# A block of zeros ahead of each landed chunk: a TensorE filler in the last message pass of a fused graph network

## The chip, the cores and the metric

The kernel runs on one core of one Trainium2 chip. The metric is the device time of one execution in microseconds (us), lower is better. The kernel before takes 6255.49 us (median of 3 runs, 6251.28 to 6260.96).

Five engines work side by side, each on its own instruction stream, and meet at semaphores: TensorE (matmuls, PE in the profile, its weight loads PEld), VectorE (DVE), ScalarE (ACT), GpSimd (POOL) and SyncE (SP), which here only issues transfers.

## The reference

Four graph layers over the same 3125 nodes of 128 features and 100000 edges, the edges sorted by destination, each followed by a residual and a layer norm:

```
x = layernorm(x + relu(three R-GCN convolutions(concat(x, type_embedding))))
x = layernorm(x + elu(layernorm(attention sums(x)) * w + b))
x = layernorm(x + (segment_sum(edge_weight * x[src], dst) @ W.T + b))            # L2
x = layernorm(x + mlp(concat(x, segment_sum(edge_attr, dst) / max(count, 1))))   # L3
```

The change touches the code that does the sums of L2 and L3, which the kernel makes in one pass over the edges.

## The kernel before, in words

Nodes are padded to 25 tiles of 128. The edges lie in chunks of 128 along the sorted destinations, and U = 6 chunks make a group. A tile of destinations is the work of several groups. A sum over the edges of a tile is a row of matmuls that accumulate in a PSUM bank: one operand is a one-hot matrix (edge by destination in the tile, times a weight), the other the 128 gathered message rows of the chunk.

There are four such message passes, numbered k = 0 to 3: one for each R-GCN convolution (k = 0, 1, 2), and the last (k = 3), which has 147 groups, 882 chunks. Passes 1 and 2 count edges between nodes as well, with four bf16 matmuls of 400 columns for each chunk (`count_sources`, L1440). Between pass 2 and pass 3 stand the attention layer and two dense stages; behind pass 3 the dense stages of the MLP.

For one group p of pass 3 the engines do this:

- GpSimd (`gather`, L493) starts one indirect DMA for each of the 6 chunks. It fetches 128 rows of `z_tab` into slot q of `msg_r`, by the row numbers in `idx_r[:, q]`. Ahead of slots 0 and 3 it waits until that half of the slots has been freed by TensorE (`s_free`) and has new row numbers (`s_idx`). There is one buffer for each slot.
- ScalarE (`rows_to_gather`, L578) waits until slot q has landed and then copies the row numbers of the next group to `idx_r[:, q]`. At a tile's end it also takes the tile's two sums out of PSUM (L686, L687).
- SyncE (L431) loads the edge attributes of the chunk into the other half of the slot once TensorE has freed it; `s_attr` tells that they landed.
- VectorE makes the group's columns (L876, L882) and then, for each half of three slots, the one-hots (`one_r`, a view of `shot_r`, L893) and the weighted one-hots (`hot_r`, L897), once the half is free.
- TensorE (`group_sums` with `chunk3`) waits at slots 0 and 3 for the one-hots (`s_hot`), at every slot for the gathered rows (`s_msg`) and the attributes (`s_attr`), and then does two fp32 matmuls: attributes by one-hots (L1580) and messages by weighted one-hots (L1581, which frees the slot). The trace lists each fp32 matmul as two matmuls with two weight loads. A tile begins with `start3` (L1575, L1576 and a clearing matmul of zeros, L1203) and ends with closing matmuls of zeros (L1207).

The accumulators of pass 3 are banks 0 to 3, two for each of two tiles in turn. `zeros_b` is a bf16 block of zeros, [128, 512], filled once at the start. Bank 5 isn't used in pass 3.

Of the kernel before, what the change touches and what calls it, by code (L numbers as in the profile page):

```python
# [18 lines left out]
P = 128  # L19
# [32 lines left out]
def build(nc, x_nodes, x_t, src_c, dst_c, typ_c, wgt_c, dst_rows, attr, node_type, emb, w1, root1, w2, root2,  # L52
          w3, b1r, b2r, emb_parts, gat_w, l2_w, m_w1, m_w2, rows, out):
    ctx = ExitStack()
    with ctx:
        def sb(name, shape, dt=F32):
            return ctx.enter_context(nc.sbuf_tensor(name, shape, dt))
# [23 lines left out]
        zeros_b = sb("zeros_b", [P, 512], BF16)  # L81
# [56 lines left out]
        psum = ctx.enter_context(nc.psum_tensor("psum", [P, 8, 512], F32))  # L138
# [1061 lines left out]
        def _(pe):  # L1200
            T = nc.tensor
# [25 lines left out]
            for n, (of, by) in enumerate(((0, ident), (1, ident), (1, before))):  # L1227
                T.matmul(psum[0:1, 6, 32 * n:32 * n + 32], rng_col[:, of:of + 1], by[0:TILES, 0:32], start=True, stop=True)
                last = T.matmul(psum[0:1, 6, 32 * n + 96:32 * n + 128], rng_wcol[:, of:of + 1], by[0:WN, 0:WN],
                                start=True, stop=True)  # L1230
# [73 lines left out]
            def transpose_relations(p):  # L1304
                pe.wait_ge(s_cols[0], p)
                T.matmul(psum[0:SPLIT * SPLIT_AT, 2, 0:P], rel_g[:, :, :].rearrange("p i n -> p (i n)"), ident_b[:, :], start=True, stop=True).then_inc(s_rel_ps, 1)

            def inverse_counts(p, slot):

                alone(pe)  # L1310
                pe.wait_ge(s_rel_t, p)
                for h in range(2):
                    T.matmul(psum[:, 6 + h, 0:UH * P], rel_t[:, :],
                             inv_b[:, bass.ds(slot, 1), h * UH * P:(h + 1) * UH * P].rearrange("p o n -> p (o n)"),
                             start=True, stop=True).then_inc(s_inv_e[h], 1)

            def group_sums(k, p, slot, chunk_sums, first=False, last=False):
                after, landed = pe.snap(p + 1), pe.snap(p * 16)
                if k == 0:
                    inverse_counts(p, slot)  # L1320
                for q in range(U):
                    if q % UH == 0:
                        pe.wait_ge(s_hot[k][q // UH], after)
                    pe.wait_ge(s_msg[k][q], landed)
                    if k == 3:
                        pe.wait_ge(s_attr[q], landed)
                    chunk_sums(q, slot, first and q == 0, last and q == U - 1).then_inc(s_free[k], 1)
                    if k == 0 and q == UH:
                        transpose_relations(after)
# [4 lines left out]
            def gathering(k, start, chunk_sums, stop, between=None, after=None, begin=1, tab=rest):  # L1334


                def tile(D, slot):
                    first, last = pe.snap(tile_range(pe, P0, D, tab)), pe.snap(tile_range(pe, LAST, D, tab))
                    start(D, slot)
                    group_sums(k, first, slot, chunk_sums, first=True)  # L1340
                    if between is not None:
                        between(D)
                    with pe.Fori(first + 1, last) as p:
                        group_sums(k, p, slot, chunk_sums)
                    group_sums(k, last, slot, chunk_sums, last=True)
                    if after is not None:
                        after(D)
                    stop(slot)

                tile(begin, begin % 2)  # L1350
                with pe.Fori(begin + 1, TILES) as D:
                    tile(D, pe.snap(D % 2))
# [292 lines left out]
```

## Time and profile before

| | |
|---|---|
| median of 3 runs | 6255.49 us (6251.28 to 6260.96) |
| the profiled execution | 6247.44 us, span of its instructions 6245.6 us |
| mean granted TensorE clock | 0.756 |
| busy share of the span | TensorE 71%, GpSimd 52%, VectorE 48%, ScalarE 17% |
| pass 0, about 730 to 2000 us | clock 0.72 |
| pass 1, about 2030 to 3140 us | clock 0.94 |
| pass 2, about 3190 to 4290 us | clock 0.95 |
| pass 3, about 4720 to 6060 us | clock 0.52 |

The span runs from the first to the last instruction. The granted clock is the share of TensorE's full rate (2.4 GHz) that it was given, and it has two levels, 0.5 and 1.0; a value between them is a mean over a stretch. Busy time is the time in which an engine had an instruction in work. Matmuls are pipelined, and the end of one is modelled, so the start of the next is the safer reading. A row of waits says for what an engine stood idle and how often. The prediction counts the passes from one: k = 1 and 2 are the second and third pass, k = 3 is the last.

### The profile page before, as it was taken

The page shows a single profiled execution, that of the slowest core. Times are in us where ns is not written, and L with a number is a line of the kernel's source. Part 1 is how long each engine was busy: PE and PEld are TensorE (multiplying, and loading weights), DVE is VectorE, ACT ScalarE, POOL GpSimd, SP SyncE. Part 2 cuts the span into 40 slices and gives each one's busy share as a digit, 9 for nine tenths or more (in the row PEclk, how much of TensorE's full clock was granted, in tenths as well). Part 3 has the DMA queues.
Part 4 walks back from the last instruction along what each step waited for, and adds up shares of the span by engine and source line. Part 5 has one row for each costly group of instructions (what it writes and reads, how often), then busy time and mean ns, then how long its engine had stood idle before and what let it go on. Part 6 is the DMA issues. An engine that isn't in the chain of part 4 may idle for free.

```text
span 6245.6 us, 98864 instructions
## 1 busy us (share of the span) xinstructions
PE 4417.3 (71%) x20570; PEld 3106.2 (50%) x20573; DVE 2981.6 (48%) x6741; ACT 1057.7 (17%) x3779; POOL 3267.3 (52%) x3114
## 2 busy tenths in 40 slices
PE   4677676767677777777767777775647777877773
PEld 1223455555565445454544444444645665666652
DVE  5443222222222666667666666666882222222235
ACT  0111111111111111111111111111751111111112
POOL 0000355555554666666666666663325666666650
PEclk7566667777777999999999999997985555555556
DMA  1011223333333122222222222222423333333320
GB/s 67 23 53 53 79 85 93 102 92 102 95 104 106 53 61 72 71 81 81 90 74 61 65 71 77 82 79 74 147 94 85 85 85 85 84 84 85 84 73 11
DMA packets 318265, 492.02 MB, mean 79 GB/s; under 512 B 98090, under 2 KB 221228, under 8 KB 314556
## 3 DMA queue, kind: packets, MB, share of 16 engines
q0 software_dynamic: 108864, 246.74, 14.6%
q1 hardware_dynamic: 209372, 244.94, 11.8%
q8 instruction: 12, 0.20, 0.0%
q14 instruction: 17, 0.14, 0.0%
HBM read 406.11 MB, written 85.29 MB: 79 GB/s over the span
## 4 chain that ended last, share of the span: by engine, by line
issue 24%; POOL 22%; PE 19%; DMA 12%; DVE 9%; another core or an unknown queue 6%; DVEq 3%; ACTq 2%; ACT 2%; POOLq 1%; SPq 0%
POOL msg_r L493 22%; DMA msg_r<-y_tab,idx_r 8%; PE psum L1375 4%; DMA msg_r<-z_tab,idx_r 3%; PE psum L1440 3%; DVE h_t L1132 2%; PE psum L1255 1%; PE psum L1580 1%; DVE hot_r L990 1%; PE psum L1287 1%; PE psum L1267 1%; PE psum L1537 1%; ACT idx_r L578 1%; PE psum L1581 1%
## 5 line engine op out<-in xcount | busy, mean ns | idle before, releaser
L493 POOL DMA_INDIRECT msg_r<-y_tab,idx_r x2160 | 2234.6, 1035 | 2053.2 <-issue 1291.3
L1440 PE MATMUL psum<-shot_r,hotb_r 128*128 128x400 bf16 x5760 | 1313.6, 353 | 573.3 <-DMA msg_r<-y_tab,idx_r 454.8
L493 POOL DMA_INDIRECT msg_r<-z_tab,idx_r x882 | 933.6, 1058 | 511.5 <-issue 323.1
L1440 PEld LDWEIGHTS psum<-shot_r,hotb_r 128*128 128x128 bf16 x5760 | 503.4, 102 | 1009.4 <-DMA msg_r<-y_tab,idx_r 489.2
L1014 DVE TENSOR_SCALAR shot_r<-iota_h,edge_g 128x1600 bf16<-128x1600 f16 x1440 | 906.1, 684 | 0.0
L578 ACT COPY idx_r<-row_i 128x1 int32 x2142 | 409.9, 191 | 2898.6 <-DMA msg_r<-y_tab,idx_r 2643.2
L1580 PE MATMUL psum<-msg_r,shot_r 128*128 128x128 f32 x1764 | 680.2, 488 | 294.3 <-DMA msg_r<-z_tab,idx_r 152.1
L1375 PE MATMUL psum<-hot_r,msg_r 128*128 128x128 f32 x2880 | 634.5, 385 | 319.8 <-DVE hot_r L990 193.9
L1375 PEld LDWEIGHTS psum<-hot_r,msg_r 128*128 128x128 f32 x2880 | 540.9, 277 | 434.3 <-issue 260.9
L1580 PEld LDWEIGHTS psum<-msg_r,shot_r 128*128 128x128 f32 x1764 | 437.2, 308 | 522.8 <-DMA msg_r<-z_tab,idx_r 351.0
L893 DVE TENSOR_TENSOR shot_r<-iota_h,dst_g 128x384 f32<-128x384 f16 x294 | 166.1, 565 | 862.7 <-PE psum L1581 436.7
L1581 PE MATMUL psum<-msg_r,hot_r 128*128 128x128 f32 x1764 | 551.3, 416 | 0.0
L893 DVE TENSOR_TENSOR hotb_r<-iota_h,dst_g 128x384 bf16<-128x384 f16 x480 | 266.5, 555 | 551.1 <-PE psum L1462 226.6
L1581 PEld LDWEIGHTS psum<-msg_r,hot_r 128*128 128x128 f32 x1764 | 474.2, 328 | 0.0
L990 DVE SCALAR_TENSOR_TENSOR hot_r<-iota,edge_g,psum 128x128 f32<-128x128 f32 x720 | 202.9, 344 | 487.0 <-remote 271.6
L578 ACT COPY idx_r<-src_i 128x1 int32 x876 | 167.6, 191 | 1145.9 <-DMA msg_r<-z_tab,idx_r 967.4
L1462 PEld LDWEIGHTS psum<-hot_r,msg_r 128*128 128x128 f32 x1440 | 278.6, 203 | 60.0 <-issue 13.6
L1495 PEld LDWEIGHTS psum<-msg_r,hot_r 128*128 128x128 f32 x1440 | 277.5, 202 | 59.0 <-issue 12.3
L1462 PE MATMUL psum<-hot_r,msg_r 128*128 128x128 f32 x1440 | 291.3, 286 | 0.0
L1495 PE MATMUL psum<-msg_r,hot_r 128*128 128x128 f32 x1440 | 290.4, 285 | 0.0
L897 DVE TENSOR_TENSOR hot_r<-hotb_r,edge_g 128x384 f32<-128x384 bf16 x480 | 283.0, 590 | 0.0
L1564 PE MATMUL psum<-side,h_t 128*128 x1250 | 170.6, 295 | 77.1 <-POOL h_t L513 52.8
(273 smaller groups left out, 3905.3 us busy)
## 6 DMA issues: line engine op xcount, KB each, us to landing
msg_r<-in_attr SPq DMA_DIRECT2D x882, 64.0 KB
h_t<-count_tab SPq DMA_DIRECT2D x25, 1600.0 KB, 6.6
count_tab<-w_s SPq DMA_DIRECT2D x48, 800.0 KB
msg_r<-y_tab,idx_r POOLq DMA_INDIRECT x2160
xn<-heavy_tab SPq DMA_DIRECT2D x76, 320.0 KB
y_tab<-y_s SPq DMA_DIRECT2D x25, 640.0 KB, 2.9
xn<-y_tab SPq DMA_DIRECT2D x25, 640.0 KB
y_tab<-y_s SPq DMA_DIRECT2D x50, 320.0 KB
```

The lines of the kernel that those rows point to most:

```text
L493: pool.indirect_dma_start(out=msg_r[:, q, 0:width], out_offset=None, in_=table, in_offset=bass.IndirectOffsetOnAxis(ap=idx_r[:, q:q + 1], ...
L578: nc.scalar.copy(idx_r[:, q:q + 1], of[:, q:q + COLS - U + 1][:, bass.ds(c0, 1)]).then_inc(s_idx[k], 1)
L893: return V.tensor_tensor(out=to, in0=iota_h[:, None, 0:P].broadcast_to(shape), in1=dst_g[:, part, None].broadcast_to(shape), op=ALU.is_equal)
L897: return V.tensor_tensor(out=to[:, half, :], in0=ones_in[:, half, :], in1=edge_g[:, plane, half, None].broadcast_to([P, UH, P]), op=ALU.mult)
L990: last = V.scalar_tensor_tensor(out=hot_r[:, q, :], in0=iota[:, 0:P], scalar=edge_g[:, DST, q:q + 1], in1=psum[:, 6 + h, (q - half.start) ...
L1014: V.tensor_scalar(out=shot_r[:, q, :], in0=iota_h[:, :], scalar1=edge_g[:, SRC, q:q + 1], scalar2=None, op0=ALU.is_equal)
L1375: last = T.matmul(acc0(slot, m), msg_r[:, q, m * P:(m + 1) * P], hot_r[:, q, :], start=False, stop=False)
L1440: ins = T.matmul(psum[:, 4 + b, 0:CB], hotb_r[:, q, :], shot_r[:, q, b * CB:(b + 1) * CB], start=first, stop=last)
L1462: return T.matmul(acc(slot), msg_r[:, q, 0:P], hot_r[:, q, :], start=False, stop=False)
L1495: return T.matmul(acc(slot), hot_r[:, q, :], msg_r[:, q, 0:P], start=False, stop=False)
L1580: T.matmul(acc(slot * 2 + 1), one_r[:, q, :], msg_r[:, q, P:2 * P], start=False, stop=False)
L1581: return T.matmul(acc(slot * 2), hot_r[:, q, :], msg_r[:, q, 0:P], start=False, stop=False)
```

## The change

In the last pass alone (k = 3), TensorE multiplies the block of zeros by itself, 128x128 weights and 512 moving columns in bf16, into bank 5, once for each slot. The matmul stands behind the wait for the one-hots and ahead of the wait for the gathered rows. It increments no semaphore, and nothing reads its result.

```diff
@@ -1321,6 +1321,8 @@
                 for q in range(U):
                     if q % UH == 0:
                         pe.wait_ge(s_hot[k][q // UH], after)
+                    if k == 3:
+                        T.matmul(psum[:, 5, :], zeros_b[:, 0:P], zeros_b[:, :], start=True, stop=True)
                     pe.wait_ge(s_msg[k][q], landed)
                     if k == 3:
                         pe.wait_ge(s_attr[q], landed)
```

## Rows read from the trace of the kernel before

**Rows 1.** The page: busy time of each engine, and the clock in 40 slices (tenths).
```profile
PE 4417.3 (71%) x20570; PEld 3106.2 (50%) x20573; DVE 2981.6 (48%) x6741; ACT 1057.7 (17%) x3779; POOL 3267.3 (52%) x3114
...
PEclk7566667777777999999999999997985555555556
```

**Rows 2.** Sums by pass: length, PE, PEld, DVE, ACT, POOL busy, clock, DMA, GB/s.
```profile
730.00:2000.00 1270.00, 902.87 (x4387) 731.76 (x4388) 316.80 (x1886) 164.86 (x767) 703.65 (x700) 0.72 0.32 97
2030.00:3140.00 1110.00, 840.22 (x4539) 545.86 (x4538) 762.19 (x1459) 181.28 (x820) 739.52 (x707) 0.94 0.25 74
3190.00:4290.00 1100.00, 809.75 (x4550) 536.24 (x4549) 751.25 (x1449) 157.47 (x746) 735.34 (x701) 0.95 0.25 72
4720.00:6060.00 1340.00, 1056.42 (x3627) 814.49 (x3626) 384.57 (x864) 175.68 (x912) 915.24 (x865) 0.52 0.31 85
```

**Rows 3.** Line 493, last pass: duration of a gather in ns, minimum/median/maximum.
```profile
L493 POOL DMA_INDIRECT msg_r<-z_tab,idx_r x865: 994/1000/1387, 4719.2 to 6059.0; - x173
```

**Rows 4.** Timeline, last pass: start and length in us, engine, line, [idle before, releaser].
```profile
5508.49 0.79 PE L1580 MATMUL psum<-msg_r,shot_r 128*128 128x128 f32 x2
...
5509.08 0.64 PE L1581 MATMUL psum<-msg_r,hot_r 128*128 128x128 f32 x2
5509.77 1.00 POOL L493 DMA_INDIRECT msg_r<-z_tab,idx_r  x1 [0.30 <-issue]
...
5511.07 1.00 POOL L493 DMA_INDIRECT msg_r<-z_tab,idx_r  x1 [0.30 <-issue]
...
5512.32 0.79 PE L1580 MATMUL psum<-msg_r,shot_r 128*128 128x128 f32 x2
...
5512.91 0.63 PE L1581 MATMUL psum<-msg_r,hot_r 128*128 128x128 f32 x2
5513.69 1.00 POOL L493 DMA_INDIRECT msg_r<-z_tab,idx_r  x1 [0.30 <-issue]
...
5516.18 0.56 DVE L893 TENSOR_TENSOR shot_r<-iota_h,dst_g 128x384 f32<-128x384 f16 x1 [5.22 <-PE psum L1581]
...
5516.95 1.25 POOL L493 DMA_INDIRECT msg_r<-z_tab,idx_r  x1 [2.27 <-ACT idx_r L578]
```

**Rows 5.** GpSimd's waits, last pass, 4720 to 6060: us in total, times, longest.
```profile
POOL msg_r L493 <- ACT idx_r L578: 127.3, 60, 2.6
POOL msg_r L493 <- PE psum L1581: 55.2, 33, 2.8
```

**Rows 6.** The same for the second pass, 2030 to 3140.
```profile
POOL msg_r L493 <- ACT idx_r L578: 107.1, 51, 3.2
POOL msg_r L493 <- PE psum L1462: 54.6, 29, 4.2
```

**Rows 7.** Timeline of TensorE in the second pass, at the full clock.
```profile
3001.20 0.85 PE L1440 MATMUL psum<-shot_r,hotb_r 128*128 128x400 bf16 x4 [0.37 <-DMA msg_r<-y_tab,idx_r]
3001.88 0.38 PE L1462 MATMUL psum<-hot_r,msg_r 128*128 128x128 f32 x2
```

**Rows 8.** Line 1203, matmuls of zeros ahead of the attention sums, ns.
```profile
L1203 PE MATMUL psum<-zeros_b x3: 314/634/634, 4379.7 to 4380.6; 128*128 128x512 bf16 x2, 128*128 128x128 bf16 x1
```

**Rows 9.** Timeline of TensorE behind a tile boundary of the last pass.
```profile
5500.37 0.63 PE L1580 MATMUL psum<-msg_r,shot_r 128*128 128x128 f32 x2
...
5501.22 0.63 PE L1580 MATMUL psum<-msg_r,shot_r 128*128 128x128 f32 x2
...
5502.33 0.49 PE L1580 MATMUL psum<-msg_r,shot_r 128*128 128x128 f32 x2 [0.19 <-DMA msg_r<-z_tab,idx_r]
5502.65 0.39 PE L1581 MATMUL psum<-msg_r,hot_r 128*128 128x128 f32 x2
```

**Rows 10.** Sums of the stretches around it (columns as in rows 2).
```profile
5497.50:5501.80 4.30, 4.30 (x21) 4.18 (x21) 0.59 (x2) 0.38 (x2) 2.62 (x3) 0.50 0.23 61
5501.90:5505.20 3.30, 0.95 (x6) 0.57 (x5) 2.39 (x6) 0.77 (x4) 1.77 (x2) 1.00 0.28 75
```

**Rows 11.** The chain of waits from 4716 to 6070, shares by line.
```profile
by line: POOL msg_r L493 34.7%; issue 31.3%; DMA msg_r<-z_tab,idx_r 15.8%; PE psum L1580 6.7%; PE psum L1581 3.8%; ACTq L578 1.9%; ACT idx_r L578 1.8%; POOLq L486 0.7%; ACTq L245 0.7%; another core or an unknown queue 0.6%; ACTq L577 0.6%; 
```

## The prediction

> **What bounds the kernel now.** I read the page first, then sums by pass, then the last pass alone. The page [rows 1] shows TensorE busy most of the time and, in the last quarter, a granted clock of only 5 tenths (1.2 GHz) where the passes before had 9. The sums by pass [rows 2] show the puzzle of this case: in the last message pass TensorE is busy 1056 of 1340 us (79%) at clock 0.52, in the second and third pass it is busy 74 to 76% at 0.94 and 0.95, and still all three take the same time for a gather: 1340/865 = 1.549 us, 1110/707 = 1.570 us, 1100/701 = 1.569 us. Nearly twice the clock bought nothing there per gathered chunk.
>
> The reason is GpSimd. One gather of the last pass takes 1.00 us [rows 3], and the next starts 0.30 us later (5509.77, 5511.07 [rows 4]), so 1.30 us is the floor: 882 x 1.30 = 1147 us of the pass. What lies above the floor are waits [rows 5]: 60 on ScalarE's index copy (127.3 us) and 33 on L1581 (55.2 us), together 93 waits and 182.5 us, 2 us each. The second pass has the same kind at the same price: 51 + 29 waits, 161.7 us [rows 6]; per gather that is 0.229 us there and 0.211 us here.
>
> What ends such a wait? In rows 4, slot 2 of a group is multiplied at 5508.49 to 5509.72. GpSimd needs that slot's release only for the gather begun at 5511.07, and is busy with the one before until 5510.77: about 1.0 us of slack. The next half group is the one that stalls, 2.27 us, until 5516.95. The chunk whose slot it needs (slot 5 of the same group) started at 5512.32 and its last matmul ended at 5512.91 + 0.63 = 5513.54, before GpSimd had even issued the gather before (5513.69 to 5514.69). So the multiply was not late; the release reached GpSimd, ScalarE and VectorE (VectorE started L893 at 5516.18) some 2.6 us after its matmul. The profile puts the wait down to ScalarE's index copy, which follows the landing of the gather begun at 5513.69: the stall ended when the last gather under way had landed. A faster matmul moves none of this. I read most of the 93 waits so.
>
> **The change, part by part.** Nothing is removed or moved. Six matmuls of 128x512 bf16 zeros with their weight loads are added to each of the 147 groups, 882 in all, into bank 5, which nothing in this pass reads (it accumulates in banks 0 to 3).
>
> Size of one: at the full clock four matmuls of 400 columns step at (3001.88 - 3001.20)/4 = 0.17 us [rows 7], so 512 columns take 0.22 us, and at half the clock 0.43 us; the row with the same form lists 0.63 us for one alone [rows 8], drain included. Added work: 882 x 0.43 = 379 us cold, 882 x 0.22 = 194 us warm, more than the pass's 284 us of idle TensorE only if everything stayed cold.
>
> What hides it: supply is one chunk in 1.30 us. Back to back a cold chunk takes 0.85 us (L1580 at 5500.37, again at 5501.22 [rows 9]), so 0.45 us are free and 0.43 us go in. Alone, from its landing, a cold chunk takes 5508.49 to 5509.72 = 1.23 us, of which the first part is the weight load, which can run under the zeros.
>
> What it does to the clock: behind a tile boundary, from 5497.5 to 5501.8, TensorE ran back to back at 0.50, and right behind it, at 5501.9, the clock was 1.00 [rows 9, 10]. With the zeros in, a cold pass is always back to back (0.85 + 0.43 = 1.28 of 1.30 us). That zeros count as work I take from the second and third pass: there most columns are one-hots against one-hots, nearly all zeros, and the clock is 0.94. I expect 0.8 to 0.95 in the last pass. A warm chunk takes 5502.33 to 5503.04 = 0.71 us [rows 9] where a cold one takes 1.23 us, so each release comes 0.52 us earlier.
>
> What that is worth:
> - The 60 ACT waits and the steady state: nothing, by the paragraph above. If the cover were gone (gathers faster than 1.28 us), each chunk would cost up to 0.43 us.
> - The 33 waits on L1581: bounds 0 and 33 x 0.52 = 17 us. A few of them look like matmuls in a row with GpSimd behind them, others like the stall above; I take half, -8 us.
> - More instructions on a warm TensorE: the second and third pass have 4539/707 = 6.4 matmuls a gather, this one 4.2, and cost 0.020 us more a gather, 18 us over 882. One more matmul of those 2.2 would be 8 us; VectorE's extra work there may be all of it, so the bounds are 0 and 18 us and I take +4 us.
> - The tail: the last chunk ends 0.5 us earlier, and a tile's close too: -1 us.
> Sum -5 us. The profiled execution took 6247.4 us around its span of 6245.6, 8 us (0.13%) under the median of 6255.5; -5 us on it is 6242, and on the median, by which I forecast, 6250 us.
>
> The Trainium skill, "Trace Analysis", section "Matmul Optimizations", says that TensorE's power follows its utilization, so that matmuls should run back to back. The rise behind the tile boundary [rows 10] agrees; that zeros do it no run here shows yet. Taken as a recipe for time, with every matmul of the last pass at twice the rate and the gain all on the path, it would give the first rival's 6184 us; the sum does not use it.
>
> **Rivals.**
> *A, the clock reaches the path (faster).* The chain of waits gives L1580 and L1581 6.7% + 3.8% of the last pass's stretch of 1354 us [rows 11], 142 us. If these are true steps, halving the matmuls takes 71 us: 6184 us. If only the stalls on L1581 vanish, 55 us: 6200 us. For it: the chain and 55.2 us of waits. Against: the second and third pass have the warm clock and as many waits.
> *B, zeros do not raise the clock and are in the way (slower).* At 0.50 the chunk plus zeros needs 1.28 of 1.30 us, so the backlog that a tile boundary leaves no longer drains. The boundary's own two fp32 matmuls are worth a chunk, 0.85 us, and its three small zero matmuls some 0.35 us (an estimate from the 0.43 us of one with 512 columns): 1.2 us behind, against 1.0 us of slack. 25 tiles x (0.2 + 0.43) = 16 us; if each of the 93 waits is lengthened by 0.43 too, 40 us more. Between 16 and 56 us I take the middle, +35 us: 6290 us. It decides from the point where the clock stays below about 0.6. Against: the zeros-heavy columns of the second and third pass.
> *C, warm, but the waits become those of the second and third pass (slower).* There a gather costs 0.020 us more than here, and in the second pass 0.018 us more of it is waiting. With TensorE as warm and fuller, the term of +4 us becomes its upper bound of 18 us and the -8 us nothing: 18 - 1 = +17 us, 6272 us. It decides if the stall comes from TensorE's instruction rate. Against: with 4.2 matmuls a gather instead of 6.4 the difference is that small, and VectorE alone can be its cause.
> *D, the clock does not rise, and all is hidden.* Then nothing changes: 6255 us. It falls within my forecast's own range.
>
> **How the numbers follow.** A measurement of this kernel (6251 to 6261) can tell about 0.2% (12.5 us) from no change. Forecast with D 0.53, own range 6240 to 6267; A 0.25; B 0.11; C 0.11. Faster 0.25, same 0.53, slower 0.22. For 8 in 10, I go down to A's smaller price, 6200 (about 0.1 is left below), and up to 6285 (C's price with 13 us over it, and B's lower end of 6271; about 0.08 is left above). 6250 is that of the likeliest case.
>
> **What the profile after should show.** The last pass's clock at 0.8 or more; 882 more TensorE matmuls; L1581's and L1580's spacing halved in most groups; GpSimd's gathers still 1.30 us apart with stalls of about 2 us every 9 to 12 gathers, on ScalarE's copy more than on L1581; the pass within 10 us of its length. The forecast is wrong if the number of stalls changes clearly: fewer would mean that TensorE's releases, held back as they look, depend on how busy or fast it is (A), more that added instructions feed the stall (C). A clock near 0.5 with longer waits on L1581 would be B.

## The result, and the profile after

The changed kernel takes 6270.28 us (median of 17 runs, 6255.65 to 6278.24), the kernel before 6255.49 us beside it. The ratio is 1.0021, with a 95% interval of 1.0013 to 1.0028: slower by 14.8 us in the median (8 to 18 us by the interval), where 6250 was forecast. The profiled execution took 6275.3 us around a span of 6273.5.

The page after (lines as in [rows 1]):

```profile
PE 4325.8 (69%) x21402; PEld 2935.0 (47%) x21455; DVE 2979.0 (47%) x6741; ACT 1057.5 (17%) x3779; POOL 3255.8 (52%) x3114
...
PEclk7566666777778999999999999997988888888876
```

The sums by pass (columns as in [rows 2]; the third pass left out):

```profile
730.00:2000.00 1270.00, 898.11 (x4342) 726.88 (x4342) 315.12 (x1879) 163.84 (x763) 701.80 (x699) 0.73 0.32 96
2030.00:3140.00 1110.00, 837.86 (x4527) 544.16 (x4526) 760.86 (x1459) 180.61 (x817) 736.75 (x704) 0.94 0.25 73
...
4720.00:6060.00 1340.00, 946.56 (x4394) 632.56 (x4442) 382.11 (x854) 173.78 (x903) 894.08 (x858) 0.83 0.31 84
```

The page shows 882 more weight loads (21455 for 20573). In the last row of the sums the granted clock went from 0.52 to 0.83, and TensorE is busy for 947 us instead of 1056, with the zeros in. The other passes are as they were in clock and busy time. So the clock did what was forecast. But in the same 1340 us GpSimd began 858 gathers instead of 865.

One gather costs what it did, and the zeros are listed at 0.38 us. Line 493 in the last pass (as in [rows 3]):

```profile
L493 POOL DMA_INDIRECT msg_r<-z_tab,idx_r x858: 992/997/1382, 4719.6 to 6059.8; - x172
```

The line of the zeros:

```profile
L1325 PE MATMUL psum<-zeros_b x809: 379/379/634, 4721.9 to 6059.6; 128*128 128x512 bf16 x162
```

The time is in GpSimd's waits. Its waits in the last pass, which answer to [rows 5] (L1583 is the old L1581):

```profile
POOL msg_r L493 <- ACT idx_r L578: 113.0, 54, 2.6
POOL msg_r L493 <- PE psum L1583: 101.2, 49, 2.4
```

Those of the second pass, which answer to [rows 6]:

```profile
POOL msg_r L493 <- ACT idx_r L578: 120.2, 59, 3.2
POOL msg_r L493 <- PE psum L1464: 45.6, 28, 4.7
```

In the last pass there were 93 waits of 182.5 us; there are 103 of 214.2 us, still some 2 us each. Those put down to ScalarE fell from 60 to 54, and those put down to TensorE's last matmul rose from 33 to 49, although that matmul now comes earlier.

The whole pass, counted from its 882 gathers (from the start of the first to the end of the last; "idle" is what the gaps between gathers have beyond the usual 0.304 us; a stall is a gap over 0.9 us):

```
          pass us   gathers busy    idle   stalls
before    1365.5       933.6       164.0      93
after     1379.7       920.2       191.5     103
```

The last pass is 1379.7 - 1365.5 = 14.2 us longer in these two profiles. The idle time grew by 27.5 us, and the gathers became 13.4 us shorter in all; the last section comes back to that.

One profile is too little to take this for the 14.8 us of the result. The two profiled executions differ by 27.9 us, and the other half of that lies in passes whose code did not change. Over six profiles beside a kernel before of about 6256 us (before, the change, and the four runs of the first set below) the unchanged first pass takes 1312 to 1327 us and has 97 to 106 such stalls. So the loss is shown by the medians of many executions, and a step from 93 to 103 stalls is hardly more than what single profiles scatter by.

The chain of waits over the last pass (as in [rows 11]):

```profile
by line: POOL msg_r L493 37.3%; issue 28.7%; DMA msg_r<-z_tab,idx_r 19.1%; PE psum L1582 3.9%; PE psum L1583 2.7%; PE psum L1325 1.3%; ACT idx_r L578 1.3%; ACTq L578 1.2%; another core or an unknown queue 0.8%; POOLq L486 0.8%; ACTq L245 0.
```

The timeline of one stall (as in [rows 4]):

```profile
5501.82 0.49 PE L1582 MATMUL psum<-msg_r,shot_r 128*128 128x128 f32 x2 [0.88 <-DMA msg_r<-z_tab,idx_r]
...
5502.14 0.39 PE L1583 MATMUL psum<-msg_r,hot_r 128*128 128x128 f32 x2
...
5502.49 1.00 POOL L493 DMA_INDIRECT msg_r<-z_tab,idx_r  x1 [0.30 <-issue]
...
5504.59 0.56 DVE L893 TENSOR_TENSOR shot_r<-iota_h,dst_g 128x384 f32<-128x384 f16 x1 [4.43 <-PE psum L1583]
...
5505.10 0.49 PE L1582 MATMUL psum<-msg_r,shot_r 128*128 128x128 f32 x2 [0.32 <-DMA msg_r<-z_tab,idx_r]
...
5505.37 1.24 POOL L493 DMA_INDIRECT msg_r<-z_tab,idx_r  x1 [1.88 <-PE psum L1583]
```

A chunk now takes 0.71 us (5501.82 to 5502.53), as forecast for a warm TensorE. Its shares of the chain fell from 6.7% + 3.8% to 3.9% + 2.7%, those of the gather and its transfer rose, and the pass did not become shorter. The stall is the one of [rows 4]. VectorE and GpSimd both need the slots freed by 5502.53. VectorE starts 2.06 us later, and GpSimd 2.84 us later. A release that is due is held back.

The trace's records of semaphore updates show this directly. In the stall of [rows 4] the matmuls that release slots ended at 5512.27, 5513.54, 5514.91 and 5516.26, and the updates of `s_free` stand at 5516.08, 5516.15, 5516.21 and 5516.28, in a burst. GpSimd started 0.80 us behind the second, which is the one that it needed. In the stall above they ended at 5502.53, 5503.35 and 5504.57, the updates stand at 5504.56, 5504.63 and 5504.70, and GpSimd started 0.81 us behind the first. In the traces of after_3 and narrow1_3, from chips without these stalls (below), each of the 882 updates stands 0.014 us behind the end of its matmul, and a GpSimd that waits for one starts 0.82 us after that end.

So it goes for nearly all stalls of the pass. GpSimd waits at slots 0 and 3, where 92 of the 93 stalls before and 102 of the 103 after lie. In all of them the matmul that it needed had ended at least 1.2 us before the restart, and 87 of the 92 and 95 of the 102 restarts come 0.79 to 0.83 us behind a recorded update of `s_free` (of the other gathers at these slots 11 of 200 and 4 of 190 do). The same test with ScalarE's `s_idx` gives 2 and 0. The stalls end with TensorE's release, whichever engine the profile names, and not with a gather's landing, as the prediction read one of them. From the end of the needed matmul to the restart the median is 3.17 us before and 3.72 us after: the matmul is some 0.5 us earlier, and the release is held that much longer.

### The profile page after: what moved, and what is told of

Read it like the earlier page. It is cut to its first block, busy times and chain, and to the rows that moved or that the text cites. A ratio compares the mean times of both kernels' runs of the same rounds, so it can differ in the third digit from the quotient of the medians.

```text
span 6273.5 us, 100578 instructions
## 1 busy us (share of the span) xinstructions
PE 4325.8 (69%) x21402; PEld 2935.0 (47%) x21455; DVE 2979.0 (47%) x6741; ACT 1057.5 (17%) x3779; POOL 3255.8 (52%) x3114
## 4 chain that ended last, share of the span: by engine, by line
issue 23%; POOL 23%; PE 20%; DMA 14%; DVE 8%; another core or an unknown queue 6%; DVEq 3%; ACT 1%; ACTq 1%; POOLq 1%; SPq 0%
POOL msg_r L493 23%; DMA msg_r<-y_tab,idx_r 9%; PE psum L1377 4%; DMA msg_r<-z_tab,idx_r 4%; PE psum L1442 4%; DVE h_t L1132 2%; PE psum L1255 1%; PE psum L1287 1%; DVE hot_r L990 1%; PE psum L1267 1%; PE psum L1539 1%; PE psum L1582 1%; PE psum L1497 1%; DVE h_t L1136 1%
## 5 line engine op out<-in xcount | busy, mean ns | idle before, releaser
L493 POOL DMA_INDIRECT msg_r<-z_tab,idx_r x882 | 920.2, 1043 | 539.0 <-issue 318.1
L1582 PE MATMUL psum<-msg_r,shot_r 128*128 128x128 f32 x1764 | 494.1, 370 | 376.8 <-DMA msg_r<-z_tab,idx_r 308.4
L1582 PEld LDWEIGHTS psum<-msg_r,shot_r 128*128 128x128 f32 x1764 | 344.4, 234 | 670.5 <-DMA msg_r<-z_tab,idx_r 573.7
L1583 PE MATMUL psum<-msg_r,hot_r 128*128 128x128 f32 x1764 | 412.4, 323 | 0.0
L1325 PE MATMUL psum<-zeros_b 128*128 128x512 bf16 x832 | 381.2, 458 | 24.0 <-DVE hot_r L897 19.1
L1583 PEld LDWEIGHTS psum<-msg_r,hot_r 128*128 128x128 f32 x1764 | 341.6, 241 | 0.0
L1497 PEld LDWEIGHTS psum<-msg_r,hot_r 128*128 128x128 f32 x1440 | 280.5, 204 | 59.5 <-issue 13.0
L1497 PE MATMUL psum<-msg_r,hot_r 128*128 128x128 f32 x1440 | 292.8, 287 | 0.0
L897 DVE TENSOR_TENSOR hot_r<-hotb_r,edge_g 128x384 f32<-128x384 bf16 x480 | 281.5, 587 | 0.0
```

What stands on the lines that cost most here:

```text
L493: pool.indirect_dma_start(out=msg_r[:, q, 0:width], out_offset=None, in_=table, in_offset=bass.IndirectOffsetOnAxis(ap=idx_r[:, q:q + 1], ...
L897: return V.tensor_tensor(out=to[:, half, :], in0=ones_in[:, half, :], in1=edge_g[:, plane, half, None].broadcast_to([P, UH, P]), op=ALU.mult)
L1325: T.matmul(psum[:, 5, :], zeros_b[:, 0:P], zeros_b[:, :], start=True, stop=True)
L1497: return T.matmul(acc(slot), hot_r[:, q, :], msg_r[:, q, 0:P], start=False, stop=False)
L1582: T.matmul(acc(slot * 2 + 1), one_r[:, q, :], msg_r[:, q, P:2 * P], start=False, stop=False)
L1583: return T.matmul(acc(slot * 2), hot_r[:, q, :], msg_r[:, q, 0:P], start=False, stop=False)
```

## The experiments

Each kernel is compared with the kernel before beside it on its own chip, and times are not compared across chips. This matters, since the chips differ more than the kernels. One chip has the 2 us stalls (kernel before: 6255.98 us in one session, 6171.06 in a second). Three others have nearly none in the last pass (5609.22, 5611.27 and 5627.04 us, 10% less). For the first comparison, of the result above, the chip is not on record; its times and stalls are those of the chip with stalls.

The questions: does the clock buy anything, does added work cost by its time or by its number of instructions, and must they be TensorE's?

### First set, on the chip with the stalls

**narrow1**: the same instructions as in the change, with 8 columns instead of 512.

```diff
+                    if k == 3:
+                        T.matmul(psum[:, 5, 0:8], zeros_b[:, 0:P], zeros_b[:, 0:8], start=True, stop=True)
```

> The zeros matmul of each slot is kept but has 8 columns instead of 512: the same 882 extra instructions pairs, almost no work. Count theory (GpSimd's stall of 2 us comes more often with every instruction on TensorE's stream): clock stays at 0.52 in the last pass, stalls over 0.9 us there rise from 93 to about 103, time +13 us, 6268 us. Clock theory (the higher clock makes the stalls more frequent): 93 stalls, 6255 us. Queue theory (512 columns of zeros stand ahead of landed chunks): 93 stalls, 6255 us.

**narrow3**: three of them for each slot.

```diff
+                    if k == 3:
+                        T.matmul(psum[:, 5, 0:8], zeros_b[:, 0:P], zeros_b[:, 0:8], start=True, stop=True)
+                        T.matmul(psum[:, 5, 0:8], zeros_b[:, 0:P], zeros_b[:, 0:8], start=True, stop=True)
+                        T.matmul(psum[:, 5, 0:8], zeros_b[:, 0:P], zeros_b[:, 0:8], start=True, stop=True)
```

> Three zeros matmuls of 8 columns in each slot, 2646 extra ones with little work. Count theory: stalls in the last pass rise by about three times as many as with one, to 115 to 125, time +30 to +40 us. Clock and queue theory: little change, under +8 us.

**vector12**: nothing on TensorE; behind the one-hots of each half VectorE increments a semaphore six times, 12 in a group. It does no work.

```diff
+                        for _ in range(UH * 2):
+                            dve.sem_inc(s_go, 1)
```

> Nothing on TensorE; instead 12 increments of a semaphore nobody waits for in each group on VectorE's stream in the last pass, behind its one-hots, as many added instructions as the weight loads and matmuls of the change. If the count theory holds for any engine's instructions (a path that all share): stalls 93 to about 103, +13 us. If it holds for TensorE alone, or the clock or queue theory holds: 93 stalls, 6255 us.

**wide_half**: the 512 columns of the change at slots 0 and 3 alone, a third of the instructions.

```diff
+                    if k == 3 and q % UH == 0:
+                        T.matmul(psum[:, 5, :], zeros_b[:, 0:P], zeros_b[:, :], start=True, stop=True)
```

> The 512-column zeros only at slots 0 and 3, 294 of them instead of 882. TensorE then has 0.85 + 0.14 us of cold work in 1.30 us, so the clock should be between, 0.6 to 0.75. Count theory: a third of the change's cost, +4 us, 96 stalls. Clock theory: in proportion to the clock, +5 to +9 us. Queue theory: +4 us.

Measured, with the gathers of the last pass counted as above in one profile each (the ratios are over 6 to 17 executions):

```
            added in the pass     clock  ratio (95%)               pass us  busy   idle  stalls
before      -                     0.52   1                          1365.5  933.6  164.0    93
wide_half   294 matmuls, wide     0.64   1.0001 (0.9992 to 1.0009)  1370.9  936.5  166.5    98
vector12    1764 increments       0.52   1.001  (1.0 to 1.002)      1375.7  930.6  177.2   103
narrow1     882 matmuls, narrow   0.52   1.0020 (1.0011 to 1.0028)  1376.8  941.9  166.9   101
after       882 matmuls, wide     0.83   1.0021 (1.0013 to 1.0028)  1379.7  920.2  191.5   103
narrow3     2646 matmuls, narrow  0.52   1.0044 (1.0032 to 1.0056)  1392.8  935.4  189.6   112
```

The sums of the last pass of narrow1:

```profile
4720.00:6060.00 1340.00, 1067.83 (x4454) 843.28 (x4453) 375.92 (x856) 174.12 (x904) 915.77 (x858) 0.52 0.30 84
```

Its waits of GpSimd:

```profile
POOL msg_r L493 <- ACT idx_r L578: 95.0, 47, 2.5
POOL msg_r L493 <- PE psum L1583: 92.8, 55, 2.4
```

GpSimd's waits in the last pass of vector12:

```profile
POOL msg_r L493 <- ACT idx_r L578: 147.8, 70, 2.8
POOL msg_r L493 <- PE psum L1583: 46.2, 36, 2.0
```

narrow1 settles the main question on this chip. It has the cold clock (0.52), adds hardly any columns, and costs what the change costs: 1.0020 against 1.0021. So clock and columns together are worth nothing that these runs can tell here (each interval is some 5 us to either side). What the columns cost and what the clock gives back are not told apart by it. In this pair of profiles the gathers of the change are 22 us shorter than those of narrow1, and its idle time is 25 us longer. Three times the instructions cost more than twice as much, with 112 stalls, and a third of them can't be told from none. Of the stall counts only the 112 stands clear of the 97 to 106 that the unchanged first pass has; narrow1's 101 does not, and its profile puts 8 us of its loss into longer gathers and 3 us into idle time. That narrow1's instructions cost time is shown; that they cost it through more stalls is not. vector12 has 103 stalls as well, with TensorE's code untouched, but at a ratio whose interval touches 1.0: it leans to "any engine's instructions" and doesn't settle it. For that a larger dose was needed.

### Second set, which fell on a chip without the stalls

**vector36**: as vector12, 36 increments in a group.

```diff
+                        for _ in range(UH * 6):
+                            dve.sem_inc(s_go, 1)
```

> 36 increments of an unread semaphore in each group on VectorE's stream in the last pass, three times the 12 of before; TensorE's stream is that of the kernel before. If instructions of any engine feed the stall: stalls in the last pass 110 or more, time +20 to +30 us. If TensorE's alone do and the +5 us of 12 increments was chance: 93 to 100 stalls, under +8 us. If VectorE is only late with its one-hots: longer waits on L897 by TensorE.

**attr_half**: fewer instructions. The attributes of three slots come in one transfer, and TensorE waits for them twice in a group instead of six times.

```diff
-                    for q in range(U):
-                        sp.wait_ge(s_free[3], p * U + (q + 1))
-                        sp.dma_start(msg_r[:, q, P:2 * P], attr[bass.ds((first_chunk(sp, p * U + chunk) + q) * P, P), :])\
-                          .then_inc(s_attr[q], 16)
+                    for q in range(0, U, UH):
+                        sp.wait_ge(s_free[3], p * U + (q + UH))
+                        sp.dma_start(msg_r[:, q:q + UH, P:2 * P],
+                                     attr[bass.ds((first_chunk(sp, p * U + chunk) + q) * P, UH * P), :]
+                                     .rearrange("(u n) f -> n u f", n=P)).then_inc(s_attr[q], 16)
...
-                    if k == 3:
+                    if k == 3 and q % UH == 0:
                         pe.wait_ge(s_attr[q], landed)
```

> The kernel before, but SyncE loads the attributes of three slots with one transfer (2 in a group instead of 6) and TensorE waits for them twice instead of six times: 4 DMA issues with their register work and 4 semaphore waits fewer in each group. Count theory for any engine: fewer stalls, 93 down to 80 to 88, time -10 to -25 us. Rival (the stall comes from TensorE's matmuls alone, or from the gathers): 93 stalls, 6255 us, or slower if the attributes now land too late.

**both_half**: that, and ScalarE copies the row numbers of three slots at once, in all four passes.

```diff
-                    for q in range(U):
...
-                        act.wait_ge(s_msg[k][q], before16)
-                        nc.scalar.copy(idx_r[:, q:q + 1], of[:, q:q + COLS - U + 1][:, bass.ds(c0, 1)]).then_inc(s_idx[k], 1)
+                    for q in range(0, U, UH):
...
+                        for j in range(UH):
+                            act.wait_ge(s_msg[k][q + j], before16)
+                        nc.scalar.copy(idx_r[:, q:q + UH], of[:, q:q + COLS - U + UH][:, bass.ds(c0, UH)]).then_inc(s_idx[k], 1)
```

> As attr_half, and ScalarE copies the row numbers of three slots at once (2 copies in a group instead of 6) in all four passes. Count theory for any engine: fewer stalls in every pass, 10 to 15% fewer each, time -60 to -100 us in all. Rival: the stalls stay as they are in the passes 0 to 2, time within 20 us of before; slower if the later row numbers bind GpSimd.

**no_attr**: the matmul of the attributes is left out, so the sums of L3 are missing from the output. It takes two of TensorE's four matmuls with their weight loads from each chunk.

```diff
-                T.matmul(acc(slot * 2 + 1), one_r[:, q, :], msg_r[:, q, P:2 * P], start=False, stop=False)
```

> The last pass leaves out the matmul of attributes by one-hots (L1580), so the attribute sums are missing from the output; the attributes are still loaded. TensorE loses 4 of its 8 matmul and weight load instructions a slot. Count theory: stalls in the last pass from 93 to 75 to 85, time -15 to -30 us. Rival (a stall has to do with gathers, not with how many instructions run beside them): 93 stalls, and only the tail's 1 us.

```
before 5609.22 us   ratio (95%)                pass us  busy   idle  stalls
vector36            1.0002 (0.999 to 1.0013)    1187.2  910.2   8.7     5
attr_half           1.0027 (1.0015 to 1.004)    1200.7  914.1  18.3    16
both_half           1.0014 (1.0004 to 1.0024)   1200.5  909.6  22.7    24
no_attr             0.994  (0.9922 to 0.9957)   1155.9  887.1   0.3     0
```

On this chip the pass takes some 1190 us instead of 1370, near the floor of 882 x 1.30 = 1147 us, nearly all stalls are gone (what is left has 0.7 us beyond the 0.30), and 5292 added increments (36 in each of 147 groups) cost nothing that can be measured. no_attr gains 34 us there, which says that TensorE's two matmuls per chunk do matter where no stall covers them. Grouping the transfers (attr_half) costs 15 us; that it lies in SyncE's wait for three freed slots and TensorE's for three attribute blocks is argued only. Both thinned kernels missed my expectation of a gain, and since neither ran on the chip with stalls, what they do there stays open.

### Third set: the same doses back on the chip with the stalls

> The changed kernel once more. If the kernel before takes about 6255 us beside it (stalls of 2 us in every pass, as in its profile): ratio 1.002 again, 103 stalls in the last pass. If it takes about 5609 us beside it (a chip without these stalls, as for the last four runs): the records theory (the stall comes of the recording of instructions, and the change costs only through it) expects no loss, and since GpSimd there waits 206 times, 64 us, for the last matmul of a slot, a gain of 10 to 50 us from the warm clock, 5560 to 5600 us. The count theory without records (each instruction costs by itself) expects +13 us there too, 5622 us.

> Three narrow zeros matmuls in each slot once more. On a chip with the stalls: 1.0044 again. On one without: the records theory expects 5609 us and up to +10 us where the narrow matmuls stand ahead of a slot that has landed, with the clock still near 0.55; the count theory +27 us.

> 36 unread increments on VectorE in each group once more. On a chip with the stalls: if instructions of any engine feed them, 110 or more stalls in the last pass, +15 to +30 us; if TensorE's alone, within 8 us. On one without: 5609 us again.

> The last pass without its matmul of the attributes (the attribute sums are missing from the output) once more. On a chip with the stalls: fewer instructions, 75 to 85 stalls in the last pass, -15 to -35 us. On one without: 0.994 again, -34 us, all of it from slots freed earlier.

```
before 6171.06 us   ratio (95%)                pass us  busy   idle  stalls
after_2             1.0021 (1.0011 to 1.0031)   1358.0  928.3  161.8    98
narrow3_2           1.0046 (1.003 to 1.0062)    1372.3  935.8  168.5   107
vector36_2          1.01   (1.0085 to 1.0115)   1402.1  922.6  211.7   133
no_attr_2           1.0062 (1.0046 to 1.0078)   1375.0  903.0  204.0    82
```

The sums of the last pass (4660 to 5900) of vector36_2:

```profile
4660.00:5900.00 1240.00, 798.57 (x3252) 664.14 (x3252) 341.28 (x777) 157.57 (x818) 815.02 (x780) 0.60 0.30 82
```

Its waits of GpSimd:

```profile
POOL msg_r L493 <- PE psum L1583: 88.3, 54, 3.7
POOL msg_r L493 <- ACT idx_r L578: 85.8, 48, 2.5
POOL msg_r L493 <- remote: 45.8, 25, 2.1
```

And what TensorE waited for by VectorE's weighted one-hots:

```profile
PE psum L1582 <- DVE hot_r L897: 130.3, 54, 5.8
```

The waits of GpSimd in no_attr_2, and one of TensorE's (L1580 is the old L1581):

```profile
POOL msg_r L493 <- ACT idx_r L578: 92.3, 35, 3.6
POOL msg_r L493 <- PE psum L1580: 91.0, 32, 6.1
PE psum L1580 <- DMA msg_r<-in_attr: 280.5, 154, 6.4
```

after_2 and narrow3_2 repeat their ratios. vector36_2 has the largest effect. Increments that wait for nothing and compute nothing, on an engine that is idle most of the pass, cost 57 us (1.0%) on this chip, where I had expected 15 to 30, with 133 stalls and 50 us more idle time than after_2. On the other chip they cost nothing (1.0002).

Its stalls are of two kinds, told apart by when the matmul that GpSimd needed ended (at slots 0 and 3; "us" is their time beyond 0.304 each):

```
             release held: matmul ended      matmul late: ended
             over 1.2 us before the restart  under 1.2 us before it
after_2      94, 154 us                      3, 5 us
narrow3_2    103, 163 us                     0
vector36_2   95, 148 us                      34, 55 us
no_attr_2    43, 90 us                       38, 110 us
```

VectorE's increments added no held releases (95 for 94). What they added is 34 stalls in which TensorE itself was late, in its wait for VectorE's one-hots (54 waits, 130.3 us, where after_2 has 19 waits of 5.4 us, at the zeros). VectorE was late by its increments: the 5255 of them that the trace lists took 348.5 us, 337 over 0.6 us each, where on the other chip 5256 took 110.4 us, 21 ns each and none longer. So on this chip another engine's instructions cost time as well, but in their own stream, and not by feeding the hold on TensorE's releases.

no_attr_2 is the miss of this set. With two matmuls and two weight loads fewer for each chunk the stalls did become fewer (82), but longer (2.45 us beyond the usual 0.30 on the mean, where the other three have 1.55 to 1.63), and the kernel is 38 us slower by its ratio. The table divides it. The held releases fell to less than half, 43 with 90 us, which is what a hold that comes with TensorE's instructions would give. In their place 38 stalls of 110 us came in which the matmul was late. There TensorE waited for the attributes, which this kernel still loads, 154 times and 280.5 us, a wait that after_2 doesn't have: SyncE began a chunk's load a median 5.5 us after the matmul that frees its slot, against 1.3 us in after_2 and 0.19 us in no_attr. Why SyncE fell so far behind here isn't shown.

### Fourth and fifth set: the clock, on chips without the stalls

> The changed kernel. Beside a kernel before of about 6170 or 6255 us (chip with stalls): 1.002 again. Beside one of about 5609 us (chip without): if the change costs only through the stalls, no loss and a gain of 10 to 50 us of GpSimd's 206 waits for TensorE; if an added instruction costs by itself, +13 us.

> One narrow zeros matmul in each slot, clock not raised. On a chip with stalls 1.002 again. On one without: 5609 us, within 8 us, so that a gain of the wide zeros there is the clock's.

> Attributes loaded and row numbers copied for three slots at once. On a chip with stalls, if instructions of any engine feed them: fewer stalls in all passes, -30 to -100 us; if only TensorE's and VectorE's do: within 15 us. On one without: 1.0014 again (later row numbers).

**both_half_zeros**: both_half, with the 512 columns of zeros for each slot as in the change.

> both_half with the change's zeros in it. On a chip with stalls: +10 to +15 us over both_half, as the change over before. On one without: 10 to 50 us below both_half by the warm clock.

> The 512-column zeros at slots 0 and 3 only. Beside a kernel before of about 5610 us (chip without stalls): the clock at 0.65 to 0.75 in the last pass and -10 to -20 us, about half of the change's gain. Beside one of about 6170 or 6255 us: 1.000 to 1.001, as the first time.

**mid128_4**: the change with 128 columns.

```diff
+                    if k == 3:
+                        T.matmul(psum[:, 5, 0:P], zeros_b[:, 0:P], zeros_b[:, 0:P], start=True, stop=True)
```

> A zeros matmul of 128 columns in each slot, a quarter of the change's columns with all of its instructions. Without stalls: the clock between 0.55 and 0.7, 0 to -10 us. With stalls: 1.002, as the change and its narrow form.

```
                  before us  clock  ratio (95%)                pass us  busy   idle  stalls
after_3            5611.27   0.99   0.9935 (0.9917 to 0.9953)   1153.9  882.4   3.2     4
narrow1_3          5611.27   0.54   1.0012 (1.0002 to 1.0022)   1201.1  911.1  21.8    16
both_half_3        5611.27   0.59   1.0009 (0.9998 to 1.0019)   1203.2  911.2  23.9    23
both_half_zeros    5611.27   0.98   0.9988 (0.9976 to 1.0)      1185.9  909.8   7.8     8
wide_half_4        5627.04   0.76   0.9946 (0.9926 to 0.9966)   1185.9  907.3  10.1     8
mid128_4           5627.04   0.69   0.9981 (0.9969 to 0.9993)   1200.3  920.4  11.6     7
```

The very same changed kernel is faster here, by 37 us. The sums of the last pass (4270 to 5390) of after_3:

```profile
4270.00:5390.00 1120.00, 797.46 (x4395) 493.15 (x4441) 373.60 (x856) 173.79 (x902) 856.08 (x857) 0.99 0.37 100
```

Its waits of GpSimd:

```profile
POOL msg_r L493 <- issue: 258.1, 847, 0.4
POOL msg_r L493 <- PE psum L1583: 5.3, 9, 1.0
POOL msg_r L493 <- ACT idx_r L578: 0.8, 1, 0.8
```

Then narrow1_3:

```profile
4270.00:5390.00 1120.00, 992.13 (x4266) 790.30 (x4267) 377.07 (x823) 167.03 (x867) 849.89 (x823) 0.54 0.35 96
```

Its waits of GpSimd:

```profile
POOL msg_r L493 <- issue: 185.7, 599, 1.0
POOL msg_r L493 <- PE psum L1583: 65.8, 203, 1.5
POOL msg_r L493 <- ACT idx_r L578: 19.0, 21, 1.3
```

Then wide_half_4:

```profile
4270.00:5390.00 1120.00, 834.96 (x3699) 630.24 (x3770) 370.58 (x832) 169.37 (x879) 856.91 (x834) 0.76 0.35 98
```

Its waits of GpSimd:

```profile
POOL msg_r L493 <- PE psum L1583: 29.3, 95, 0.6
POOL msg_r L493 <- ACT idx_r L578: 10.0, 13, 1.1
```

None of these waits is of the 2 us kind. And the 203 waits on L1583 in narrow1_3 are less than they look: 65.8 us is 0.32 us each, hardly more than the 0.30 us that GpSimd needs between two gathers anyway (the 847 of "issue" in after_3 take 0.30 us each). Beyond that a cold pass is idle for 21.8 us and a warm one for 3.2: 19 us, which I put down to TensorE's earlier releases. The larger part of the 47 us between these two passes is the gathers, 911.1 against 882.4, 29 us; the last section shows what makes them longer. The change's own instructions, narrow1_3, cost a few microseconds here (1.0012, 1 to 12 us by the interval), and its columns, through the clock, bring the rest. That interval overlaps with narrow1's on the chip with stalls (1.0011 to 1.0028), so up to all of narrow1's 12.5 us can be a cost that has nothing to do with the stalls.

Three fillers in the order of their clock, 0.69, 0.76 and 0.99, give 0.9981, 0.9946 and 0.9935 (the last on another chip). both_half_zeros brings both_half_3 down by 15 us only, although its clock is 0.98: its gathers stayed at 910 us.

The versions, on both kinds of chip:

```
             with stalls                       without
the change   1.0021, 1.0021                    0.9935
wide_half    1.0001 (0.9992 to 1.0009)         0.9946 (0.9926 to 0.9966)
narrow1      1.0020                            1.0012
```

wide_half_4 gained 30 us, more than the 10 to 20 that I had expected of it. wide_half is the version to keep. It is not measurably slower than the kernel before on the chip with the stalls, and takes most of the gain on the others (the two gains are from different chips, and their intervals overlap).

## Why the prediction was wrong

The range of 6200 to 6285 held the time, but not the sign. Point by point:

- **The clock** (0.8 to 0.95 forecast): 0.83. Right, and so was the step behind it, that zeros count as work: narrow1 with its 8 columns stayed at 0.52. The forecast that a warm chunk takes 0.71 us was right to the digit. Rivals B and D, which have the clock stay down, are out.
- **Zeros hidden in GpSimd's 1.30 us**: right as far as can be told. narrow1 and the change cost the same, so the 512 columns cost nothing that the clock did not give back.
- **The 60 waits on ScalarE's copy, worth nothing**: right in value (54 of them after), wrong in what ends them. The copy of [rows 4] was long done; the restart follows TensorE's held release (87 of 92 stalls).
- **The 33 waits on L1581, "I take half, -8 us"**: failed, measured nothing (1.0021 with the warm clock against 1.0020 without). They became 49. I had read the stall of [rows 4] as a release held back, and yet let half of these waits be matmuls that come late. The price of 2 us, the same as that of the other 60, was in [rows 5] and spoke for one kind. In none of the 92 stalls at slots 0 and 3 before, and in none of the 102 after, was the matmul late; when it ended 0.5 us earlier, its release was held 0.5 us longer.
- **"More instructions on a warm TensorE", +4 us with bounds 0 and 18**: mis-sized. narrow1 gives it alone, though at the cold clock: 1.0020 of 6256 is 12.5 us (7 to 18 us), and the whole change's +14.8 us lies within its interval. With +12.5 for +4 and 0 for -8 the sum of -5 becomes +11.5; either correction alone gives +3 to +3.5, within the noise, so it took both failures to get the sign and the size wrong. The upper bound of 18 us, from the second pass's extra matmuls, was the better value; I gave VectorE the benefit of the doubt, without a row that priced its part.
- **The tail, -1 us**: not resolved by any run. Instead of staying within 10 us of its length, the last pass grew by 14.2 us in the profile.
- **What would show it wrong**: "more that added instructions feed the stall (C)". The count came, 103 stalls for 93, but the unchanged first pass differs from one profile to another by nearly as much (97 to 106), so this sign could not have decided.

Rival C, given 0.11, forecast 6272 us, and 6270.28 was measured. That added TensorE instructions cost this much is shown (narrow1). Its condition, that the stall comes from TensorE's instruction rate, agrees with the large doses: 92 held releases before and 110 in narrow3 in the first session, 94 with the change and 43 with half of each chunk's matmuls left out in the second, though there late matmuls took the place of some. At the change's own dose it isn't told from the scatter, and narrow1_3 costs 1.0012 without any such stall. That C came within 2 us is luck. Its price had counted the waits of the second and third pass, not a measured dose. Against it I had put only that the passes differ little per gather, an argument about the size of a cost of which 0.2% is all there is to find.

Rival A, the clock reaching the path for 55 to 71 us, comes true in part where there are no stalls: 37 us (after_3), and, by the profiles of after_3 and narrow1_3, more of it through gathers that get shorter (29 us), which it had not foreseen, than through TensorE's earlier releases (some 19 us). With the stalls nothing is left of it that can be measured. By the profiles of narrow1 and the change 22 us of shorter gathers were given back as 25 us of idle time; after_2 and narrow3_2 show little of the exchange (8 us shorter gathers, 7 us less idle time), so that its size is open.

What stays open: what holds the releases back, why SyncE fell behind in no_attr_2, how much of narrow1's 12.5 us is stalls, and whether the releases are held in an execution that leaves no records.

## What to carry to other kernels

Where an engine's waits all have one length, whatever releaser they are put down to, treat them as one kind of stall, and compare the end of the instruction that releases with the restart (here 3.17 us apart where 0.82 us is usual) before trusting a gain on the named releaser. Test the price of added instructions with instructions that do next to nothing (here 882 matmuls of 8 columns, +12.5 us), and take the scatter of a count from passes that did not change (here 97 to 106 stalls). A filler for the clock should have few instructions and many columns; 294 wide matmuls got 30 us where 882 got 37, and cost nothing where 882 cost 15. And repeat a result of some tenths of a per cent on another chip: the sign of this one depended on it.

## What the runs showed of the hardware that was not expected

**Chips of one type differ by 10% on one kernel, by a stall and not by a clock.** The kernel before took 6171 to 6256 us on one chip and 5609 to 5627 on three. The granted clock of the last pass is the same on both (0.52 and 0.54 in narrow1 and narrow1_3). The gaps between gathers account for the difference: beyond 0.30 us each they hold 879 us over the four passes in the trace of the kernel before and 242 us in that of vector36, 637 of the 640 us between the two executions, and the gathers take as long on both. The stalls go together with two other marks in the records. The trace of the kernel before lists 36509 semaphore updates and that of the change 36256, while vector36, after_3 and narrow1_3, on chips without stalls, list 83491 to 88653, so that most are missing where the stalls are. And short sequencer operations (register moves, arithmetic, comparisons) that otherwise take some 40 ns took 640 to 760 ns 470 times in the trace of before and 413 times in that of the change, and never in those of the other chips. They are mostly SyncE's (336 and 312), and in the last pass of no_attr_2 there are 778 for 153 in after_2. A path that records and releases share, and that now and then is full, would fit all three marks and a dependence on the number of instructions. No run shows this, and narrow3, with the most TensorE instructions, has fewer slow operations in its last pass than before (128 for 257). The Trainium skill, "NOTIFIC — the notification-queue block", section "7.1 Overflow: three behaviours, one of which stalls the engine", says that the block that writes the records never drops one inside itself but holds back the engine that produces it. That would be such a path, though it would not by itself account for the missing updates; no run here has the records turned off or reads the block's count of stalls.

**Zeros at 71% busy hold the clock at 0.99, and real fp32 matmuls at 89% leave it at 0.54.** These are after_3 (797 of 1120 us busy) and narrow1_3 (992 of 1120). no_attr, at 62%, had 0.50. The busy share of the profile says little about the clock that is granted.

**A gather is longer where VectorE's L897, which reads two SBUF tiles, starts in its middle.** A stretch of the timeline of after_3:

```profile
4902.59 0.56 DVE L893 TENSOR_TENSOR shot_r<-iota_h,dst_g 128x384 f32<-128x384 f16 x1 [2.72 <-PE psum L1583]
4903.11 1.00 POOL L493 DMA_INDIRECT msg_r<-z_tab,idx_r  x1 [0.30 <-issue]
...
4903.18 0.56 DVE L897 TENSOR_TENSOR hot_r<-shot_r,edge_g 128x384 f32<-128x384 f32 x1
```

And of narrow1_3:

```profile
4906.84 0.56 DVE L893 TENSOR_TENSOR shot_r<-iota_h,dst_g 128x384 f32<-128x384 f16 x1 [3.13 <-PE psum L1583]
4906.89 1.38 POOL L493 DMA_INDIRECT msg_r<-z_tab,idx_r  x1 [0.30 <-PE psum L1583]
...
4907.44 0.56 DVE L897 TENSOR_TENSOR hot_r<-shot_r,edge_g 128x384 f32<-128x384 f32 x1
```

Where L897 starts 0.4 to 0.6 us into a gather, the gather takes 1.35 us on the mean (67 of them in narrow1_3, 2 in after_3); where it starts in the first 0.2 us, 1.00 us (251 in after_3), and where it starts 0.6 to 0.8 us into it, 1.00 us again (169 in narrow1_3). A warm TensorE frees the slots earlier, VectorE begins earlier against the gather, and the overlap falls where it is harmless: 10 gathers over 1.1 us in after_3, 101 in narrow1_3. These long gathers (over 1.1 us) hold 31.7 us beyond 1.00 us each in narrow1_3 and 2.6 in after_3, the 29 us by which the busy time of the two passes differs. The Trainium skill, "GPSIMD Engine Reference", section "1. Specifications", lists GpSimd's SBUF interfaces as shared with VectorE, with contention against VectorE instructions that have two SBUF inputs. The pairing agrees, but that a start early or late in the gather does no harm is nothing that the page tells of. The order in time is read from the traces; no run moved VectorE alone to test it.
